# An AdaLN block on one core: batch 0's attention order, its output-weight split, and the order of the feed-forward's first norm

## What is computed

```
h   = layernorm(x) * (1 + ca) + sa
q, k, v = h @ wq, h @ wk, h @ wv      # 32 query heads and 8 key/value heads of 128; rope on q and k
attn    = softmax(q k^T / sqrt(128), rows i - 255 .. i only) v
x   = x + ga * (attn @ wo)            # ga and gb kept at least 0.25 from zero
h   = layernorm(x) * (1 + cb) + sb
p   = softmax(h @ gate_w^T); the two largest of 8 experts, their weights scaled to sum 1
out = x + gb * sum over experts e of weight_e * (h @ lora_A[e]^T) @ lora_B[e]^T
```

## Time and profile before

| | |
|---|---|
| median of 3 runs | 2665.49 us (2664.18 to 2667.14) |
| profiled execution, its own time | 2667.07 us |
| its span in the trace | 2665.3 us |
| mean granted clock of PE, share of full speed | 0.993 |
| group 0's first V matmul | at 87.91 us |
| group 8's first V matmul (batch 1) | at 700.70 us |
| batch 2's, group 16 | at 1285.74 us |
| last output projection, half 4 | at 2427.88 us |
| first product with lora_A | at 2452.30 us |

### The profile page before, as it was taken

How to read it: one execution, slowest core, us unless ns; L and a number is a source line. 1 busy time by engine, 2 the same in 40 slices (tenths; PEclk the granted TensorE clock), 3 DMA queues, 4 the chain that set the end, 5 groups by cost and what they waited for, 6 DMA issues and landing times.

```text
span 2665.3 us, 40308 instructions
## 1 busy us (share of the span) xinstructions
PE 2602.6 (98%) x12873; PEld 2158.9 (81%) x12873; DVE 1594.9 (60%) x4151; ACT 1154.2 (43%) x2582; POOL 250.5 (9%) x120
## 2 busy tenths in 40 slices
PE   5999999999999999999999999999999999998999
PEld 3778787888888888888888888888888888886887
DVE  3766666666766565556656665556566665546553
ACT  3555555454344443333444443333444443335441
POOL 2323333332000000000000000000000000000122
PEclk8999999999999999999999999999999999999999
DMA  7667755558654444435545543347455555546221
GB/s 279 257 218 260 259 201 199 193 196 321 230 181 148 140 160 159 157 143 217 194 173 181 181 151 125 131 153 280 180 179 198 212 189 221 186 167 243 100 80 56
DMA packets 175640, 499.78 MB, mean 188 GB/s; under 512 B 15088, under 2 KB 57392, under 8 KB 174000
## 3 DMA queue, kind: packets, MB, share of 16 engines
q1 hardware_dynamic: 170352, 479.61, 49.8%
q10 hardware_dynamic: 5184, 18.88, 1.8%
HBM read 376.76 MB, written 121.67 MB: 187 GB/s over the span
## 4 chain that ended last, share of the span: by engine, by line
PE 76%; issue 15%; POOL 6%; DVE 1%; DMA 1%; ACT 1%; SPq 0%; POOLq 0%; DVEq 0%; ACTq 0%
PE bank L632 23%; PE bank L634 23%; PE bank L633 23%; PE bank L697 4%; POOL w_q_lo L602 3%; POOL w_o_lo L602 2%; DMA stage<-in_wv 1%; POOL w_k_lo L602 1%; PE bank L1638 0%; PE bank L248 0%; PE bank L725 0%; DVE rotated L1050 0%; POOL w_v_lo L602 0%; DMA wm<-in_wmod 0%; PE bank L1651 0%
## 5 line engine op out<-in xcount | busy, mean ns | idle before, releaser
L632 PE MATMUL bank<-w_o_hi,qo_hi 128*128 128x512 f32 x1024 | 409.2, 400 | 0.9 <-DVE acc L1067 0.7
L632 PE MATMUL bank<-hT_hi,w_q_hi 128*128 128x512 f32 x1024 | 400.8, 391 | 0.2 <-DVE swapped L1047 0.2
L634 PE MATMUL bank<-w_o_hi,qo_lo 128*128 128x512 f32 x1024 | 399.9, 391 | 0.0
L633 PE MATMUL bank<-w_o_lo,qo_hi 128*128 128x512 f32 x1024 | 398.8, 389 | 0.0
L634 PE MATMUL bank<-hT_hi,w_q_lo 128*128 128x512 f32 x1024 | 398.7, 389 | 0.0
L633 PE MATMUL bank<-hT_lo,w_q_hi 128*128 128x512 f32 x1024 | 398.7, 389 | 0.0
L874 ACT ACTIVATE prob<-prob,nbias 128x384 f32<-128x384 f32 (+2 forms) x512 | 273.5, 534 | 130.6 <-DVE nbias L1080 119.9
L1080 DVE CUSTOM_DVE_ANT_0 prob<-bank,mask_t 128x384 f32<-128x384 f32 (+2 forms) x512 | 231.2, 453 | 144.8 <-PE bank L634 92.0
L1046 DVE TENSOR_TENSOR rotated<-bank,cos_t 128x512 f32<-128x512 f32 x160 | 110.6, 691 | 310.5 <-ACT swapped L858 308.4
L951 ACT ACTIVATE pT_hi<-bank 128x384 fp32r<-128x384 f32 (+2 forms) x512 | 203.8, 405 | 185.0 <-PE bank L697 179.6
L1067 DVE TENSOR_TENSOR acc<-bank,acc 128x512 f32<-128x512 f32 x256 | 173.8, 688 | 182.1 <-PE bank L634 182.1
(11 more groups left out here) (207 smaller groups left out, 4772.6 us busy)
## 6 DMA issues: line engine op xcount, KB each, us to landing
w_q_hi<-w_q_hi_scratch SPq DMA_DIRECT2D x96, 512.0 KB, 8.2
w_q_lo<-w_q_lo_scratch SPq DMA_DIRECT2D x96, 512.0 KB, 8.9
w_o_hi<-w_o_hi_scratch SPq DMA_DIRECT2D x96, 512.0 KB, 7.8
w_o_lo<-w_o_lo_scratch SPq DMA_DIRECT2D x96, 512.0 KB, 8.4
stage<-in_wq SPq DMA_DIRECT2D x32, 512.0 KB, 5.2
stage<-in_wo SPq DMA_DIRECT2D x32, 512.0 KB, 5.3
w_q_hi_scratch<-w_q_hi SPq DMA_DIRECT2D x32, 512.0 KB, 6.4
w_q_lo_scratch<-w_q_lo SPq DMA_DIRECT2D x32, 512.0 KB, 7.1
```

What stands on the lines that cost most here:

```text
L632: eng.matmul(o, st[0], mv_[0], start=start, stop=False)
L633: eng.matmul(o, st[0], mv_[1], start=False, stop=False)
L634: return eng.matmul(o, st[1], mv_[0], start=False, stop=stop)
```

## The change

Batch 0 takes the common loops: `pe_groups(eng, 0, True, False)` and `dve_groups(eng, 0, True, True)` replace `K_SPLIT`, `dve_split_groups` and the `fill` arguments. So its key steps stand at units 0 to 7, halves 0 to 3 of the output projection inside the attention, and DVE's order is that of the other batches, with four subtractions more per group. The chunks are renumbered: 0 to 3 the query weight, 4 the value weight, 5 the next key weight, 6 to 9 the output weight. POOL subtracts only 0 to 5; DVE takes 6 to 9 (`dve_chunk`, semaphore s_osplit):

```diff
+        def dve_chunk(eng, n, j):
+            slot, dst, src = chunk(j)
+            eng.wait_ge(s_hi, 10 * n + j + 2)
+            eng.tensor_tensor(dst[1], src, dst[0].bitcast(F32), ALU.subtract).then_inc(s_osplit, 1)
...
-        def dve_rope(eng, n, r, early=True, between=lambda: None):
+        def dve_rope(eng, n, r, split=False):
...
                 for u in range(EARLY):
                     dve_mask(eng, n, u)
+                if split:
+                    dve_chunk(eng, n, NC - 1)
             eng.wait_ge(s_proj, 6 * n + 2 + r)
...
                     dve_normalise(eng, n, u)
-            between()
+            if split and 1 < r < GQ:
+                dve_chunk(eng, n, 5 + r)
...
             eng.tensor_tensor(lo, rotated[slot][:], hi.bitcast(F32), ALU.subtract).then_inc(s_qk, 1)
+            if split and r == 1:
+                dve_chunk(eng, n, 6)
```

So DVE's chunk 6 stands at the end of rope 1, 7 and 8 between sum and lo of ropes 2 and 3, and 9 at the start of rope 4 behind two masks. ACT makes chunks 0 and 1 at the end of the attention, ahead of the last `act_outputs`; chunk 6 goes behind rope 1 (7, 8 and 9 stay where they were), and the norm tile's eight steps are spread over ropes 1 and 2:

```diff
+        def act_first_chunks(eng, n):
             for j in (0, 1):
                 act_chunk(eng, n, j)
+        def act_project_split(eng, n, tile=None):
             act_rope(eng, n, 0, True)
             act_chunk(eng, n, 2)
+            act_chunk(eng, n, 3)
             if tile is not None:
                 act_tile_sqrt(eng, tile)
-            for j in (3, 4, 5):
-                act_chunk(eng, n, j)
-            for r in range(1, 1 + GQ):
+            act_chunk(eng, n, 4)
+            act_chunk(eng, n, 5)
...
+            act_rope(eng, n, 1, True, lambda: act_tile(eng, tile, range(0, 2)))
+            act_tile(eng, tile, range(2, 6))
+            act_rope(eng, n, 2, True, lambda: act_tile(eng, tile, range(6, KT)))
+            act_tile_hi(eng, tile)
+            for r in (3, 4):
                 act_rope(eng, n, r, True)
```

SP issues each load ahead of the stores, the norm tile's store ahead of those of chunks 6 and 7, and at the batch's end the reload of the next batch's input ahead of the last two stores:

```diff
+        KEEP_AT = {4: (0,), 5: (1, 2), 6: (3, 4), 7: (5,)}
+        def sp_split_group(eng, n, before_q=lambda: None, tile_store=lambda: None):
...
+            for j in range(2):
+                sp_chunk(eng, n, j)
+                sp_keep(eng, NC - 2 + j, n - 1)
+            before_q()
+            for j in range(2, NC):
+                sp_chunk(eng, n, j)
+                for i in KEEP_AT.get(j, ()):
+                    keep(i)
+            tile_store()
+            for i in (6, 7):
+                keep(i)
```

```diff
             for r in range(1 + GQ):
-                dve_rope(eng, 0, r, False)
+                if r == GQ:
+                    eng.wait_ge(s_md[0], 64)
+                dve_rope(eng, 0, r, split=True)
...
-            for u in range(LA):
-                pe_scores(eng, 0, u)
-            pe_project(eng, 0, "V", w_v, slice(0, HD), 1, {})
+            pe_v(eng, 0, False)
...
+        def pe_v(eng, n, direct):
             eng.wait_ge(s_wor, 8 * n + 1)
             for u in range(EARLY):
                 pe_scores(eng, n, u)
             bank_free(eng, n, "V")
```

In the feed-forward the first norm's chunk 0 goes ahead of half 4, and the others behind the halves by twos; DVE's order follows, ACT's copy of the gate weight moves from chunk 0 to chunk 3, a wait moves from chunk 0 to chunk 1, and the last batch's loads of x and ga go from ACT's queue to SP's, behind the gate weight:

```diff
+        BESIDE_WO = {4: (1, 2), 5: (3, 4), 6: (5, 6), 7: (7,)}
...
         def p2_pe(eng):
+            pe_ln2_chunk(eng, 0, 0)
             for half in range(FILL, 8):
-                pe_wo(eng, LAST, half, True, True)
-                pe_ln2_chunk(eng, 0, half - FILL)
+                pe_wo(eng, LAST, half, True)
+                for k in BESIDE_WO[half]:
+                    pe_ln2_chunk(eng, 0, k)
             for t in range(BATCH):
                 for q in range(2):
-                    if t == 0:
-                        pe_ln2_chunk(eng, 0, 4 + 2 * q)
-                        pe_ln2_chunk(eng, 0, 5 + 2 * q)
                     pe_gate(eng, t, q)
```

More of the change, by code:

```diff
@@ L173, in p0_act @@
             for r in range(1, 1 + GQ):
-                act_rope(eng, 0, r, True, False)
-            for u in range(EARLY):
-                act_exp(eng, 0, u)
+                act_rope(eng, 0, r, True)
         def sp_store_gate(eng, q, row):
@@ L587, in act_chunk @@
             slot, dst, src = chunk(j)
-            if j == 0:
+            first = isinstance(n, int) and n == 0
+            if j == 0 and not first:
+                eng.wait_ge(s_proj, 6 * n)
+            elif j == 4:
                 eng.wait_ge(s_proj, 6 * n + 1)
@@ L593, in act_chunk @@
                 eng.wait_ge(s_wo, 8 * n + 1)
-            if not (isinstance(n, int) and n == 0):
+            if not first:
                 eng.wait_ge(s_ws[j], 32 * n)
@@ L615, in p1_pool @@
             first_chunk(eng, True)
-            for j in range(NC):
+            for j in range(6):
                 pool_chunk(eng, 0, j)
@@ L619, in p1_pool @@
             plain(eng.memset(acc[:], 0.0)).then_inc(s_acc0, 1)
[L620 to L624, removed]
+            with eng.Fori(1, KV) as n:
+                for j in range(6):
                     pool_chunk(eng, n, j)
@@ L654, in pe_tile, with wo_bank, pe_wo @@
             m.then_inc(s_lt, 1)
-        def wo_bank(half, fill):
-            return bank[1] if fill and half < FILL else SBANK[half % 3]
-        def pe_wo(eng, n, half, fill, direct):
+        def wo_bank(half):
+            return bank[1] if half < FILL else SBANK[half % 3]
+        def pe_wo(eng, n, half, direct):
             t, c = divmod(half, 2)
@@ L742, in pe_attention @@
                     pe_values(eng, n, u // GQ - 1)
[L743 to L746, removed]
+                if u in WO_AT:
+                    pe_wo(eng, n, WO_AT.index(u), o_direct)
             pe_values(eng, n, QT - 1)
@@ L858, in act_rope @@
             eng.activation(swapped[slot][half:HD, :], bk[0:half, :], ACT.Copy).then_inc(s_act, 1)
-            if split and 1 <= r < GQ:
+            if split and 1 < r < GQ:
                 act_chunk(eng, n, 5 + r)
-            if r == GQ and early:
+            if r == GQ:
                 for u in range(EARLY):
                     act_exp(eng, n, u)
+            between()
             dst = kt_[0][:] if r == 0 else qo[0][:, r - 1, :]
@@ L866, in act_rope @@
             eng.activation(dst, rotated[slot][:], ACT.Copy).then_inc(s_rh, 1)
-            if split and r == GQ - 1:
-                act_chunk(eng, n, NC - 1)
+            if split and r in (1, GQ - 1):
+                act_chunk(eng, n, 6 if r == 1 else NC - 1)
         def act_exp(eng, n, u):
@@ L929, in act_tile, with act_tile_hi, act_attention @@
                 ins.then_inc(s_laf, 1)
-                eng.wait_ge(s_laf, i + 2)
-                eng.activation(l_hi[:], lf[:], ACT.Copy).then_inc(s_lhi, 1)
-        def act_attention(eng, n, b, more=True):
+        def act_tile_hi(eng, i):
+            eng.wait_ge(s_laf, i + 2)
+            eng.activation(l_hi[:], lf[:], ACT.Copy).then_inc(s_lhi, 1)
+        def act_attention(eng, n, b, more=True, tail=lambda: None):
             for s in range(UNITS + LAG):
@@ L958, in act_attention @@
                     act_last(eng, s)
+            tail()
             act_outputs(eng, n, QT - 1)
@@ L1004, in p1_act @@
             act_groups(eng, last, False)
-            act_load_x(eng, last, range(QT))
-            act_load_ga(eng, last)
         def act_groups(eng, b, ln):
@@ L1066, in dve_wo @@
             a = acc[:, t, cc * 512:(cc + 1) * 512]
-            eng.tensor_tensor(a, wo_bank(half, fill)[:], a, ALU.add).then_inc(s_wor, 1)
+            eng.tensor_tensor(a, wo_bank(half)[:], a, ALU.add).then_inc(s_wor, 1)
         def dve_outputs(eng, n, i):
@@ L1251, in p1_dve, with dve_group @@
             dve_groups(eng, last, False)
-        def dve_group(eng, n, b, part=None):
+        def dve_group(eng, n, b, part=None, split=False):
             dve_attention(eng, n - 1, b)
@@ L1444, in p2_act @@
                 act_ln2_chunk(eng, 0, k)
-                if k == 0:
+                if k == 3:
                     eng.wait_ge(u_g, 32)
@@ L1587, in res @@
                 dve_residual(eng, BATCH - 1, LAST_ORDER[at], BATCH + 1, at)
-            for half in range(4, 8):
+            dve_h2(eng, 0, 0)
+            for half in range(FILL, 8):
                 dve_wo(eng, LAST, half)
-                dve_h2(eng, 0, half - 4)
-            for k in range(4, KT):
-                dve_h2(eng, 0, k)
+                for k in BESIDE_WO[half]:
+                    dve_h2(eng, 0, k)
             res(0)
```

209 lines of the change are left out of this document (88 added, 121 removed).

## The result

The changed kernel takes 2650.87 us (2649.44 to 2653.07, 5 runs) against 2665.49: ratio 0.9947, interval [0.9932, 0.9961]. It is faster, as forecast, but by 14.6 us where 33 were forecast; 2632 is missed, and so is the range of 2626 to 2646.

What follows compares the result with a forecast made beforehand. PE was busy 98% of the span, so time could only come from where PE stands. Batch 0's 23.35, the prologue's 4.2 and the tail's 5.5 made 33.05 us, giving 2632 us, range 2626 to 2646.

Steps and rivals of the forecast that it cites:

- SP's order: Loads go ahead of stores on SP, so loads come no later: cost 0, bounds ±0.3 us per group.
- the staging chain: Batch 0's loads, ACT's hi and the lo parts, timed from Q0, with a load landing 5.3 us after issue.
- rival (d): Slower: batch 0's staged loads become the bound; 6.9 us a leg costs 33 us, all the gain; chance 0.04.
- the 23.35: Batch 0's gain in us: 27.75 less 4.0 for tile groups and 0.4 for other groups and the batch's last.
- The attention's order: Batch 0: halves 0 to 3 fill the turns' waits; 1.86 us gained per plain group, bounds 0 to 1.86.
- The split: Four subtractions per group move from POOL to DVE at 1.22 us each; held additions return up to 6.3 us.
- Rival (a): Batch 0's tile groups: the attention's late start stays, losing 11.8 us in place of 4.0; 2640 us, chance 0.22.
- Rope 2's sine: Batch 0, behind chunk 6 on DVE: comes at 16.8 us, Q3 due at 17.2, hidden with 0.4 to spare.
- wrong altogether: Sign: Q3 waits over a microsecond for rope 2's sine in each group; chunk 6's DVE place costs the order's gain.
- The prologue: V follows the second score product, starting at 83.7 instead of 87.91: 4.2 us gained, bounds 0 and 4.4.
- The tail: Half 4 to lora_A's product, 24.42 us before, gets shorter by 5.5 us, bounds 3.2 and 6.3.

Runs made afterwards that it cites:

- one_store_each: The changed kernel with one pair of stores behind each load from 4 to 9, instead of two pairs behind loads 5 and 6: 2636.25 us, ratio 0.9883.
- stores_last: The changed kernel with all stores of split parts behind the group's last staged load: 2641.32 us, ratio 0.9901.
- prologue_only: The kernel before with only the prologue's end changed (V behind two score products, first masks in rope 4): 2665.95 us, ratio 0.9995.
- first_chunks_late: Changed kernel, stores behind all loads (groups 1 to 6) or one pair per load (group 7), ACT's chunks 0 and 1 behind attention's last output copy: 2644.93 us.

## Why the prediction was wrong

**The step that failed** is "SP's order": "The loads come no later by this", cost 0, and with it the leg of 5.3 us in the staging chain, taken from a kernel that put one pair of stores behind a load. With two pairs, legs 5 and 7 took 6.8 and 9.0 us in the tile group shown. This is the place of rival (d), whose sign came: ACT idle for staged loads, and landings near 7 us. Its price was for 6.9 us on every leg, all of the gain, and its chance 4 in 100; leg 9 ran at 3.5 in that group and at 4.4 in the plain one, and batch 0 came 18 us short, a good half of the forecast gain and not all. Give the loads the landing that the chain assumed, and the sum nearly holds: one_store_each, with 5.2 us, is 31.0 us below its own runs of before where 33.05 was said, with batch 0 giving 19.9 of the 23.35. That the whole comes nearer than this term is partly chance, since V's start alone varies by some 3 us (see the prologue below). With 3.5 us the kernel is 36.6 us below. There was a sign to read: the kernel before already had its DMA engines at 0.93 while a tile group's loads ran.

```profile
282.00:305.00 23.00, 23.00 (x107) 19.13 (x106) 13.25 (x24) 7.77 (x10) 12.42 (x6) 1.00 0.93 328
```

**Point by point.**

- *The attention's order.* The turns' waits went as said, but 0 was wrong as its lower bound: alone the order costs 49 us. It pays only together with parts that the prediction gave no price of their own, ACT's early chunks above all. That the new chunk order is another of them is what the wait for the last query chunk suggests; it wasn't tried alone.
- *The split.* It was right: 1.22 us a piece, and the additions no longer held. Rival (a) is out, since the first turn of a tile group waits 0.3 us and not 1.8; and the two runs on POOL show that the owner of the pieces matters, by 28 and 16 us. The rule of the Trainium skill on the shared port ("Perfetto Trace Analysis", Optimizing Scalar/DVE Operations) says that a move between GpSimd and DVE might not help. The additions held up in kernels with ten pieces on POOL (maxima of 2782 and 2777 ns) agree with its reason; here the move did help, with DVE taking half as long for a piece.
- *Rope 2's sine.* "0.4 us to spare, and any microsecond that chunk 6 is later beyond that is lost one for one": the load of chunk 6 took 7.3 us instead of 5.3, and Q3 waited 1.07. The sign "wrong altogether" came in the four tile groups, where Q3 waited 1.07 to 1.73 us, but not for the reason given with it: it wasn't chunk 6's place on DVE, since with the same place and early landings (stores_last) no Q3 of groups 1 to 7 waits, but ACT's wait for the load ahead of rope 2's copies.
- *The prologue.* V started at 82.95 (said 83.7). But prologue_only has V as early, at 82.54, and gives it back in group 0, so the 4.2 us are no gain of that part alone; which other part keeps them, no run separates. Among the kernels with the new prologue V started between 80.54 and 83.45, among those with the old one between 85.2 and 87.91, so the 4.96 of these two traces holds up to some 3 us of chance.
- *The tail.* 5.62 in the trace and 5.4 alone, said 5.5; the last gate half waits 0.41 us, and no stretch at the lower clock is left there. (The pitch of 0.23 us for a gate matmul isn't half of 0.40, but the matmuls do start 0.23 us apart in the changed kernel.)
- *Not foreseen.* 1.2 us in group 16, where ACT stands 1.61 us ahead of a copy for nothing that the profile shows; why stays open.

## What to carry to other kernels

A transfer's time from issue to landing belongs to the traffic around it: before its median goes into a chain, read the DMA share of the stretch, and count the bytes that the new order puts ahead of it. Stores that nobody waits for for tens of microseconds belong behind the last load of the chain, unless another load that is waited for (here the reload at the batch's end) stands behind them in the same queue. An engine that works in order passes the lateness on: here PE's waits named DVE, DVE's named ACT, and only ACT's named the load. And parts of a change that free each other's waits have no prices of their own: the order alone lost 49 us, the prologue alone gained nothing that could be told.

## What the runs showed of the hardware

The 512 KB staged load landed in 3.5, 5.2 and 7.3 us (medians of the output weight) as none, one and up to two pairs of 512 KB stores were issued with each load; in the last case the DMA engines were at 1.03 of their span and moved 394 GB/s in the stretch shown. With the stores on ACT's queue, issued somewhat later, it was 6.1. In all kernels that ran ten of POOL's 2.4 us subtractions per group the longest rope addition on DVE was 2.77 to 2.89 us; in all that ran six it was 0.69 to 0.70. Six pieces are no guard by themselves: in first_chunks_late, which runs six, rope 0's sine product still took 2.56 us beside one of them.
